# A decoder layer on one core: every step of a hand-placed timetable placed again, score transposes by head, the last output tile in quarters

## The reference, cut to what matters

```
x = layernorm(x + attention(x))      # 16 heads of 32, causal, scores clipped by the mask, softmax over keys
x = layernorm(x + wkv(w, u, x, ctx)) # a scan over the 512 positions, in each of 512 channels
x = layernorm(x + ffn(x))            # silu(x Wg) * (x Wu), then Wd, 2048 inner features, weights kept as integers
```

## Time and profile before

| | |
|---|---|
| median of 3 runs | 736.61 us (734.54 to 737.92) |
| the profiled execution's own time | 737.51 us |
| its span in the trace | 735.6 us |
| PE busy | 709.8 us, 96% |
| DVE, ACT, POOL busy | 499.6, 427.3, 294.6 us |
| granted PE clock | 0.997 of full speed |

### The profile page before, as it was taken

The page is one execution under the profiler, slowest core; times in us unless marked ns, Lnnn a source line. Parts: engine busy times, 40 slices in busy tenths (PEclk is TensorE's granted clock), DMA queues, the critical chain, the costliest instruction groups (busy, mean ns, idle before and its releaser), DMA issues.

```text
span 735.6 us, 11840 instructions
## 1 busy us (share of the span) xinstructions
PE 709.8 (96%) x4178; PEld 385.3 (52%) x4178; DVE 499.6 (68%) x1162; ACT 427.3 (58%) x1019; POOL 294.6 (40%) x321
## 2 busy tenths in 40 slices
PE   8898999999999999998999999998999999999996
PEld 3465666565655665665544454444544454444442
DVE  3567677698999985899626899959567653532233
ACT  5689787888888777879656753064513533023310
POOL 2014124167564324532345854477434732023310
PEclk9999999999999999999999999999999999999999
DMA  7535874553413153543044010000000000000001
GB/s 250 173 92 124 249 232 123 147 141 101 102 58 105 40 159 101 112 86 77 1 75 98 0 58 15 29 15 1 0 29 29 0 1 1 30 29 1 1 14 44
DMA packets 45531, 54.17 MB, mean 74 GB/s; under 512 B 4896, under 2 KB 34848, under 8 KB 45472
## 3 DMA queue, kind: packets, MB, share of 16 engines
q1 hardware_dynamic: 41632, 46.59, 21.1%
q0 software_dynamic: 3264, 6.29, 5.0%
q10 hardware_dynamic: 576, 0.52, 0.3%
HBM read 47.10 MB, written 12.58 MB: 81 GB/s over the span
## 4 chain that ended last, share of the span: by engine, by line
PE 72%; DVE 10%; ACT 7%; DMA 4%; issue 3%; POOL 3%; SPq 0%; ACTq 0%; POOLq 0%; DVEq 0%
PE psb L823 25%; PE psb L711 8%; PE psb L749 7%; PE psb L836 5%; PE psb L834 5%; PE psb L794 5%; PE psb L727 5%; PE psb L762 4%; PE psb L738 3%; ACT ee L921 2%; PE psb L810 2%; DVE x L1141 2%; DVE ek L1167 2%; PE psb L782 2%; PE psb L773 1%
## 5 line engine op out<-in xcount | busy, mean ns | idle before, releaser
L1070 DVE CUSTOM_DVE_ANT_0 ee<-psb,mask,clip 128x512 f32<-128x512 f32 (+3 forms) x256 | 130.1, 537 | 21.2 <-PE psb L738 20.6
L921 ACT ACTIVATE ee<-ee,nm 128x512 f32<-128x512 f32 (+3 forms) x256 | 142.3, 559 | 1.9 <-DVE nm L1070 1.8
L1384 POOL TENSOR_TENSOR hl<-hf,hh 128x512 f16<-128x512 f32 x64 | 77.9, 1217 | 107.9 <-ACT hh L996 107.9
L932 ACT ACTIVATE ee<-psb 128x512 f32<-128x512 f32 (+1 forms) x172 | 90.1, 524 | 45.1 <-PE psb L749 26.4
L996 ACT ACTIVATE hh<-hf 128x512 bf16<-128x512 f32 x64 | 40.3, 630 | 122.3 <-DVE hf L1194 117.5
L749 PE MATMUL psb<-ident,ee 128*128 128x128 f32 x640 | 101.3, 274 | 6.1 <-ACT ee L921 4.8
L1194 DVE SCALAR_TENSOR_TENSOR hf<-th,c,psb 128x512 f32<-128x512 f32 x60 | 43.8, 730 | 81.4 <-PE psb L823 64.1
L823 PE MATMUL psb<-x2h,wg 128*128 128x512 f16 x256 | 97.1, 379 | 1.9 <-DVE hf L1194 1.0
L836 PE MATMUL psb<-wd,hl 128*128 128x512 f16 x256 | 97.0, 379 | 0.0
L823 PE MATMUL psb<-x2h,wu 128*128 128x512 f16 x256 | 97.0, 379 | 0.0
L823 PE MATMUL psb<-x2l,wu 128*128 128x512 f16 x256 | 97.0, 379 | 0.0
(11 more groups left out here) (121 smaller groups left out, 1203.5 us busy)
## 6 DMA issues: line engine op xcount, KB each, us to landing
qs<-parts SPq DMA_DIRECT2D x64, 128.0 KB, 2.9
ks<-parts SPq DMA_DIRECT2D x60, 128.0 KB, 3.3
parts<-qhl SPq DMA_DIRECT2D x16, 256.0 KB, 2.4
parts<-khl SPq DMA_DIRECT2D x16, 256.0 KB, 2.3
x<-in_x SPq DMA_DIRECT2D x4, 1024.0 KB, 7.7
ct<-in_ctxT SPq DMA_DIRECT2D x4, 1024.0 KB, 6.3
out<-x SPq DMA_DIRECT2D x16, 256.0 KB, 2.0
xt<-in_xT SPq DMA_DIRECT2D x14, 256.0 KB, 3.6
```

The costliest lines, as they stand in the source:

```text
L921: e.activation(dst, dst, ACT.Exp, bias=NM[:, n % 4, col:col + 1], scale=-1.0, accum_out=DEN[:, n % 4, col:col + 1]).then_inc(sem("exp"), 1)
L932: e.activation(ET[h][:, base:base + width], PSB[:, bank["turn", H, item], 0:width], ACT.Copy).then_inc(sem("et"), 1)
L1070: e.tensor_tensor_reduce(E[H % 3][:, EOFF[i]:EOFF[i] + w], PSB[:, bank["score", H, i], 0:w], MASK[:, S - w:S], -SC, CLIP[:, i:i + 1], ALU. ...
L1384: e.tensor_tensor(HS[it][1][:], ring(b, it)[1][:], HS[it][0][:], ALU.subtract).then_inc(sem("hl"), 1)
```

## The change

Four things are changed.
- The tables get new numbers: nearly every slot, the waits, the DMA issues' slots, `TURN` (now by head and item), `COPIES`. 36 of the 192 score copies are on DVE instead of 20. `KEYS` is all 0: batch 2's `ekv` products move from POOL to DVE.
- `OH_POOL` and `XH_POOL` are set for 9 of 16 groups and for batches 1 to 3: POOL makes these 9 `oh` and 12 `xh` tiles (`tensor_scalar` by 1.0) that ACT made. The code for it stood in the kernel before.
- The last output tile `y(3, 3)` is made as four quarters of 128 columns, each in a PSUM bank of its own, with multiply, residual and statistics for each quarter.
- `bn_aggr` of that tile combines four statistics.

```diff
-EARLY_AT = (244, 254)
+EARLY_AT = (246, 256)
-WAIT = {'high': 1, 'low': 1, 'vtake': 1, 'r1': 0, 'norm': 5, 'exp': 3, 'eb': 0, 't1': 1, 't3': 0, 'oh': 2, 'ol': 2,
-        'ek': 1, 'scan_q': 1, 'scan_p': 6, 'divide': 8, 'r2': 2, 'x2h': 0, 'x2l': 0, 'expand': 0}
+WAIT = {'high': 1, 'low': 1, 'vtake': 1, 'r1': 2, 'norm': 4, 'exp': 4, 'eb': 0, 't1': 0, 't3': 0, 'oh': 2, 'ol': 2,
+        'ek': 1, 'scan_q': 3, 'scan_p': 6, 'divide': 8, 'r2': 2, 'x2h': 1, 'x2l': 3, 'expand': 0}
-KEYS = (0, 0, 1, 0)
+KEYS = (0, 0, 0, 0)
-TURN = ((2, 3, 4), (2, 3, 4), (2, 3, 4), (2, 3, 4))
+TURN = ((4, 6, 5), (3, 4, 6), (3, 6, 5), (3, 4, 4))
-OH_POOL = (0, 0, 0, 0, 0, 0, 0, 0, 0, 0, 0, 0, 0, 0, 0, 0)
-XH_POOL = (0, 0, 0, 0)
+OH_POOL = (1, 1, 0, 1, 0, 1, 1, 1, 0, 0, 0, 1, 0, 1, 1, 0)
+XH_POOL = (0, 1, 1, 1)
-COPIES = (0, 4, 1, 2, 2, 0, 0, 0, 0, 0, 0, 0, 0, 0, 0, 1)
+COPIES = (5, 2, 0, 4, 1, 1, 0, 0, 0, 0, 0, 2, 2, 0, 0, 1)
...
+    def y_quarters():
+        for q in range(4):
+            tt.unit("y_cut", q)
+            add("y_cut", q)
+            add("yd_cut", q)
+            add("r3_cut", q)
+        add("aggr_cut")
...
+            for it in range(IT):
+                pe.wait_ge(*by("hh", b, it))
+                e.matmul(PSB[:, bk, 0:P], HS[it][0][:, rows], wd[:, it, cut], start=(it == 0), stop=False)
+                pe.wait_ge(*by("hl", b, it))
+                mm = e.matmul(PSB[:, bk, 0:P], HS[it][1][:, rows], wd[:, it, cut], start=False, stop=(it == IT - 1))
...
+            e.tensor_tensor(YS[:, 1, cut], PSB[:, bank["y_cut", q], 0:P], DS[:, cut], ALU.mult).then_inc(sem("yd_cut"), 1)
...
+            e.tensor_tensor(x, YS[:, 1, cut], x, ALU.add).then_inc(sem("r3_cut"), 1)
+            dve.wait_ge(*by("r3_cut", q))
+            e.bn_stats(ST4[:, q, :], x).then_inc(sem("bs_cut"), 1)
```

More of the change, by code:

```diff
@@ new lines @@
+WAIT_IN = {'r1': 6, 'norm': 2, 'ek': 1, 'scan_q': 1, 'scan_p': 1, 'divide': 2, 'r2': 0, 'x2h': 2, 'x2l': 2}
+PIECE_AT = {'load_second': 41, 'small': 101, 'split_wo': 46, 'load_ds': 229}
+WU_AT = (41, 71, 77, 116)
+WU_ZERO = (83, 88, 137, 144)
+WG_AT = (207, 207, 214, 215)
+WG_ZERO = (224, 235, 241, 244)
+REST_AT = (16, 41, 97, 72)
+BO_AT = (41, 97, 129, 197)
+XLOAD = {1: (0, 6, 19, 31), 2: (45, 68, 76, 85), 3: (134, 134, 150, 164)}
+XSPLIT = {1: (17, 25, 41, 45), 2: (84, 91, 97, 100), 3: (149, 153, 156, 162)}
@@ new lines @@
+WKV_AT = {(0, 0): 111, (0, 1): 123, (0, 2): 133, (0, 3): 143, (1, 0): 191, (1, 1): 209, (1, 2): 262, (1, 3): 264,
+          (2, 0): 266, (2, 1): 272, (2, 2): 274, (2, 3): 277, (3, 0): 288, (3, 1): 292, (3, 2): 294, (3, 3): 297}
+YT_AT = {0: (156, 164, 174, 183), 1: (269, 270, 270, 270), 2: (283, 283, 286, 287), 3: (302, 303, 303, 308)}
+X2_AT = {0: (225, 228, 230, 232), 1: (272, 272, 272, 273), 2: (290, 291, 291, 292), 3: (314, 314, 314, 314)}
+WO_IN = (10, 11, 11, 14)
+ZERO_IN = (8, 9, 11, 12, 12, 12, 12, 14, 14, 14, 14, 14, 14, 14, 14, 14)
@@ L163 @@
     "y": lambda b, t: ("yd", b, t),
+    "y_cut": lambda q: ("yd_cut", q),
     "score": lambda H, i: ("weigh", H, i),
@@ L330, in y @@
         late(1, lambda: last(b, t))
+    def y_quarters():
[5 more added lines that the diff above has]
+        add("aggr_cut")
+        add("rstd", 2, B - 1, T - 1, T)
+        late(1, lambda: last(B - 1, T - 1))
     def last(b, t):
@@ L504, in timetable @@
         for t in range(T):
-            y(b, t)
+            if (b, t) == (B - 1, T - 1):
+                y_quarters()
+            else:
+                y(b, t)
             for u in extra.get(256 + 20 * b + IT + t, ()):
@@ L826, in gate_up, with y_cut @@
                 mm.then_inc(sem(name), 1)
+        def y_cut(q):
+            bk, cut, b, rows = bank["y_cut", q], slice(q * P, (q + 1) * P), B - 1, slice((T - 1) * P, T * P)
+            emptied(("y_cut", q))
+            for it in range(IT):
[3 more added lines that the diff above has]
+                mm = e.matmul(PSB[:, bk, 0:P], HS[it][1][:, rows], wd[:, it, cut], start=False, stop=(it == IT - 1))
+            mm.then_inc(sem("y_cut"), 1)
         def y(b, t):
@@ L882, in _ @@
                 y(*a)
+            elif name == "y_cut":
+                y_cut(*a)
     @block.scalar
@@ L1214, in _, with yd_cut, r3_cut @@
         e.memset(wol[:, 0, :], 0.0).then_inc(sem("zeros"), 1)
+        def yd_cut(q):
+            cut = slice(q * P, (q + 1) * P)
+            dve.wait_ge(*by("y_cut", q))
+            dve.wait_ge(sem("r3"), 4 * B - 2)
+            e.tensor_tensor(YS[:, 1, cut], PSB[:, bank["y_cut", q], 0:P], DS[:, cut], ALU.mult).then_inc(sem("yd_cut"), 1)
+        def r3_cut(q):
+            cut = slice(q * P, (q + 1) * P)
+            x = X[B - 1][:, T - 1, cut]
+            dve.wait_ge(*by("yd_cut", q))
+            e.tensor_tensor(x, YS[:, 1, cut], x, ALU.add).then_inc(sem("r3_cut"), 1)
+            dve.wait_ge(*by("r3_cut", q))
+            e.bn_stats(ST4[:, q, :], x).then_inc(sem("bs_cut"), 1)
         for name, *a in tt.order:
@@ L1217, in _ @@
                 split_w(*a)
+            elif name == "yd_cut":
+                yd_cut(*a)
+            elif name == "r3_cut":
+                r3_cut(*a)
+            elif name == "aggr_cut":
+                dve.wait_ge(sem("bs_cut"), 4)
+                e.bn_aggr(MV[:, 2 * B + B - 1, T - 1, :], ST4[:]).then_inc(sem("ba2"), 1)
             elif name == "scale_bqk":
```

35 lines of the change are left out of this document (10 added, 25 removed).

## The result

The changed kernel takes 728.25 us (median of 4 runs, 727.72 to 728.83), the kernel before beside it 735.78 us (4 runs, 734.54 to 737.92): ratio 0.9895, 95% interval 0.9868 to 0.9922, so faster by 1.1%. Run again in the study it took 727.5 us against 737.96, ratio 0.9872 (0.9848 to 0.9896). The forecast of 728.1 us was right as a number. As an account of where the time comes from it was right for the last tile and for the ffn's net gain, and wrong on where the waits for `exp` lie, on what caused the ffn's stops and on the high halves.

The account below looks back on a forecast made before the run. PE was taken as the bound nearly everywhere, DVE from 330.4 us for 17.5 us. Terms summed to -7.9, with turn stops -8.5 us, so the 736.6 median becomes 728.1; the forecast's own range is 724 to 732.5, the whole reaches 736.5.

Parts of the forecast that it names:

- The start: To 23.5 us: pieces before the first score keep their order, so the change gives 0.
- Turns: Long attention stretch, 23.5 to 330.4 us: later turns close most stops for `exp`, 3.0 of 5.5 us, plus 0.16 per stop.
- 330 to 375 us: DVE-bound stretch and attention's end: the first's 3.0 us idle stays, 1.5 of the 2.6 behind it goes.
- The ffn of batch 1: 435.3 to 530.6 us: moved pieces and `KEYS` take 3.4 us idle and four stops of 0.16, 4.0 gained.
- The last tile: Last output tile in quarters: 1.2 us less DVE work at the end, 0.26 more on PE, net gain 0.9.
- GpSimd's high halves: 21 tiles go from ACT to POOL at 0.63 us each; PE may feel it in places, 0.5 us charged.
- POOL and DVE disturb each other: POOL's new work lengthens DVE's by 1 to 2 us, hidden but in groups 7 to 9; 0.5 us charged.
- `pv` behind the last turn: `pv` stands 1.6 us of PE work behind the last turn in half the groups, before 2.1; 0.5 us charged.
- DVE becomes the bound: Rival, groups 7 to 15 and tiles `y(0, t)`: half of DVE's added 13.8 us lands on PE, median 742.6; chance 0.07.
- weight loads bound the quarters: Rival, last tile: loads at 0.098 us each cost 5.4 us more, median 733.5; chance 0.06.
- POOL late: Rival: high halves late by 1.2 us at `qk` of three batches and `wo` of batch 2, median 732.9; chance 0.05.
- The attention's stops only move: Rival: none of the attention's 11 us goes, ffn and last tile as forecast, median 733.2; chance 0.18.

Follow-up runs that it names:

- the even table: The changed kernel with every head's turns at slots 3, 4 and 5: ratio 1.0036 of the kernel before, 12.0 us slower than the changed kernel.

## Why the prediction was right, and where it wasn't

The sum was -8.5 us; the first measurement's medians show -7.5, the second's ratio -9.4, and the profile that the sum was made against is 9.4 us longer than that of the changed kernel. That 728.1 met 728.25 so closely is partly luck: the median of before was 736.61 when the forecast was made and 735.78 beside the changed kernel, and terms that were missed in opposite directions nearly cancel. By its steps:

- *The start, 0.* The fourteen profiles have 4.4 to 6.9 us of stops there, with the old tables and the new. The first profile of the changed kernel had 1.2 more than that of before, the second 0.2.
- *Turns, -3.0 and -0.64 for the stops.* The term was placed in the long stretch, where PE waited only 1.3 us for `exp`; the other 3.5 of the 4.8 us that the earlier trace rows give lay behind 330.4. Groups 0 to 13 gained 2.9 us, some 0.8 of it luck, so the size was near and the reason wrong. Nor does the later place bring a gain by itself: turns alone cost 6.9 us, and in the changed kernel, against the even table, they are worth 12. A later turn takes PE's wait for `exp` away (0.4 us is left with the turns alone), but it moves the copy, `weigh` and `pv` behind it, and only the other tables make room for these.
- *330 to 375 us, -1.5.* Measured -3.1 (0.6 in group 14, 2.4 in group 15), twice the term. It fits the five waits for `exp` there, 3.5 us, of which 0.6 is left in one stop (a score's wait of 0.5 for `exp` is new). That most of group 14's stops stay, as DVE is full there, was right. That the last turns would still wait for the last `exp` wasn't: these stops (0.3 and 0.9 us before) are gone, and one of 0.8 us for a copy on DVE stands there.
- *The ffn of batch 1, -4.0.* Measured -5.3, and +1.0 for `wo(3, 3)`, which now stands behind a turn whose bank `x`'s residual (L1157) must empty, and which I hadn't seen. The net of -4.3 is the term. But the step that read the earlier trace rows as a th that is late "between two table loads" failed: 3.8 of the 5.3 us go with the four `ekv` products alone, and the placements that I had made responsible add 1.5. The placements without `KEYS` weren't run, so what they would give by themselves is open.
- *The last tile, -0.9.* 2.18 to 0.98 us on DVE, 6.91 to 7.15 on PE, 1.0 in sum, and 0.9 to the end of the span in the run with the quarters alone. In the changed kernel 0.6 is left of it: the aggregate takes 0.26 us where it took 0.18, and from the norm's end to the span's end it is 2.7 us where it was 2.4. The quarter's three instructions took 0.284, 0.292 and 0.294 us, the statistics' estimate of 0.285 among them. The Trainium skill's 81 ns at 128 columns ("TensorE: Matmul & The Clock Gate", "Back-to-back issue gap") doesn't hold here: 0.056 us with a new load for each matmul.
- *GpSimd's high halves, +0.5.* Wrong in sign and nearly ten times too small: 4.7 us in its favour. Its own time was right, 0.62 us a tile (forecast 0.63). What was missed is what ACT gets: I had priced the engine that takes the work and not the queue that it leaves, where the waits for copies are 2.5 us shorter with it. The table of copies, at nothing by the forecast, matters by 5.9 us; PE's waits for ACT's copies don't change with it, so the reason is open.
- *POOL and DVE disturb each other, +0.5.* The second scan of the earlier trace rows now takes 1215/2223/2228 ns (min, median, max): the maximum is the same, and more scans reach it. Two of POOL's products grew (`ct` 1.76 to 2.01 us, `ek` 1.47 to 1.80), while `ol` fell from 1.38 to 1.16. But POOL's new work isn't what did it: with the ffn's tables alone eleven of 16 scans take 2.22 us or a little more, with the high halves back on ACT ten, and with the attention's tables alone, high halves and all, none takes more than 2.08. So what counts is beside which product a scan is placed. The rule of "SBUF — State Buffer", section "SBUF: two separate sides", in the Trainium skill, that the one of the two that comes second waits until the other is done, fits the scans' limits of 1.21 and 2.23 us; no run here isolates it. No wait of PE names a scan, so the 0.5 that I charged isn't shown.
- *`pv` behind the last turn, +0.5.* PE waits 0.6 us once for it.

The table of stages sorts the rivals. "DVE becomes the bound", "weight loads bound the quarters" and "POOL late" didn't come. But the last is real: it is what the same POOL work does in the old placement (2.7 us, 4.1 with the turns). "The attention's stops only move" is what the turns and ACT's relief do by themselves; all the attention's tables together do close stops.

What I had announced: PE idle under 3 us between 23 and 330 us was missed (4.8). 1.5 us of it is a wait for `ks` at 61.9 us that is new; without it 3.3 would be left. The cause of that wait is an edit that I had left unpriced: `REST_AT`'s first slot, 60 to 16, puts 1 MB in front of `qs` and `ks`; the four `ks` then take 6.1 to 7.1 us to land where they took 3.0 to 3.4. I had listed such a wait as a sign of a wrong prediction; as one of 0.9 us at 122 us is gone, it was 0.6 us more in sum. The rest came: under 1.5 us in batch 1's ffn, no wait for ACT above 1.0 us ahead of group 14, the quarters' 0.056, the tail's 1.0.

What stays open is how much of the copies' 5.9 us is ACT's relief, and what the moved load would cost at a third place. Turns of before in the new placement weren't tried.
